# Key tiles of 128 tokens instead of 112, through device memory

## Chip, cores and metric

The kernel runs on one core of a Trainium2 chip. The time is device microseconds (us) of one execution; less is better.

## What is computed

The input is 32 images of 56 x 56 pixels with 32 channels. Three parts follow each other, each with a residual sum:

```python
x = x + conv(binarize(batchnorm(groupnorm(x))))        # 3 x 3, weights reduced to their signs
t = tokens(x)                                          # 3136 tokens of 32 channels an image
t = t + attention(layernorm(t))
t = t + experts(layernorm(t))                          # best 2 of 8, weighted

# attention, 16 heads of 32:
q = elu(n @ wq.T + bq) + 1;  k = elu(n @ wk.T + bk) + 1;  v = n @ wv.T + bv
kv_cos = sum over tokens of (k * cos)^T v;  kv_sin = sum over tokens of (k * sin)^T v
out = (q * cos @ kv_cos + q * sin @ kv_sin) / (q * cos . sum(k * cos) + q * sin . sum(k * sin) + 1e-5)
out @ dense.T + dense_b
```

The sum over tokens in kv_cos and kv_sin is the part that the change cuts anew: a sum does not care in which order or in which tiles the tokens come.

## The kernel before

**Tiles.** An image's 3136 tokens are kept as four groups g (the parity of row and column), each of 7 tiles of 112 tokens: 28 slots of 112. Token tiles lie with 112 partitions; channel tiles lie with 4 x 32 = 128 partitions.

**Stages.** Five engines each walk a list of steps; step kinds have short names, and a step n of image m waits on semaphores for what it reads. For one image: XT turns the loaded pixels to channels on partitions (DVE makes the signs in `nat`); CV shifts `nat` by DMA and convolves; XC centres and turns back to tokens; POOL's PN1 makes the normed tokens `xn` (L785 and L789); ZT turns `xn` on PE in two halves, ACT keeps the fp16 high part and DVE the low part (L684, L971), and the queue of SP copies the parts into the four partition groups of `z1`, 16 DMAs in SBUF (L470).

K (L551) is 14 steps an image, each two matmuls of 112 tokens against 512 key columns; ACT makes the exponential (L688) and DVE the elu (L975) into `kbuf`, of which there are two. KX (L560) is 14 steps, each two fp32 matmuls of `xcs` (the normed tokens times cos and sin, made by POOL's CS, L797, from `xn`) with `kbuf`; it adds up over the image in one PSUM bank. G and `KT` make the small matrices from it. Then Q, DN, SU, R, RP, NM and T2 (queries, denominators, numerators, L576 to L624), PN2 and ZU (the second norm, with 16 more DMAs into `z2`), LG (router), RT and GT (gates), F (experts: L636, DVE's product L1058, three POOL sums L841 to L847) and OUT.

**Order.** The order of the steps is a table, worked out by a planner beforehand. `ORDER` gives each engine, for each step kind, a time for each n in units of which 14 are one image; `iteration` sorts an engine's steps by that time modulo 14, with the image that each belongs to, and that list repeats for each image. The times fix only the order within one engine: an engine that waits holds back everything behind it in its list. PE's results go through three PSUM slots of two banks (K, Q, R, RP, F, ...) and one bank (XT, CV, DN, NM, T2, ...); a slot is reused when its reader is done. The queue of SP has its own list: OUT, ZT, CV, XT (load of the next image), ZU.

**Opening.** Group norm and batch norm need sums over all images. SP loads all 32 images in 8 pieces of four into two stage buffers (L423, L429), PE turns them (L495), DVE gathers statistics (L891), and a chain over PE, DVE and POOL makes the thresholds. Then all weights (L433) and tables (L439) are loaded, and before its list PE waits for `act_pre`, which ACT sets after it has written a folded weight into `p2` (L654), itself after all tables are in. POOL waits for all weights and tables and prepares the fp16 weights.

## Time and profile before

| | us |
|---|---|
| median of 3 runs | 2426.46 |
| lowest and highest | 2424.11, 2431.5 |
| profiled execution, its own time | 2426.23 |
| its span, first to last instruction | 2424.4 |
| mean granted clock of TensorE | 0.961 of full speed |

The span is cut from the first to the last instruction of the core; the time of the execution has 1.8 us around it. PE is TensorE's matmuls, PEld its weight loads, DVE VectorE, ACT ScalarE, POOL GpSimd, SPq the queue of SyncE, which only issues DMAs. L551 is line 551 of the kernel.

### The profile page before, as it was taken

The numbers are of one execution on the slowest core, as the hardware profiler recorded it, in microseconds if no ns is written. First come the engines' busy times: TensorE is split into PE (matmuls) and PEld (weight loads), VectorE is DVE, ScalarE is ACT, GpSimd is POOL, SyncE is SP. The second block draws the span as 40 slices with busy tenths as digits, with TensorE's granted clock in tenths as the row PEclk, the third lists the DMA queues.
The fourth block names the chain that finished last, engine by engine and source line by source line (L and its number), as shares of the span: only waits on it lengthen the run. The fifth ranks groups of instructions, "written<-read, shape, count | busy, mean of one in ns | idle before, by whom it ended". The sixth has DMA issues, their size and how long they took to land.

```text
span 2424.4 us, 45391 instructions
## 1 busy us (share of the span) xinstructions
PE 2252.8 (93%) x15908; PEld 1126.0 (46%) x15908; DVE 2064.4 (85%) x2725; ACT 1589.9 (66%) x2789; POOL 1841.0 (76%) x1553
## 2 busy tenths in 40 slices
PE   4369999999999999999999999999999999999971
PEld 4324444444544444444544444454544444454441
DVE  5357899999999999999999999999999999998852
ACT  0157777777777777777777777777777777777620
POOL 0414588888888888888888888888888888888775
PEclk8589999999999999999999999999999999999985
DMA  7421112222221112222221212222211212211001
GB/s 209 112 39 22 32 29 44 35 42 45 45 44 34 36 34 43 34 44 44 45 42 36 34 37 40 35 45 45 45 39 37 37 36 40 36 38 35 21 21 27
DMA packets 284863, 105.31 MB, mean 43 GB/s; under 512 B 246032, under 2 KB 279680, under 8 KB 284512
## 3 DMA queue, kind: packets, MB, share of 16 engines
q1 hardware_dynamic: 284640, 102.41, 21.3%
q8 instruction: 131, 2.15, 0.4%
q14 instruction: 92, 0.75, 0.1%
HBM read 31.19 MB, written 12.85 MB: 18 GB/s over the span
## 4 chain that ended last, share of the span: by engine, by line
PE 67%; DVE 15%; ACT 6%; issue 5%; POOL 3%; DMA 2%; SPq 1%; POOLq 0%; DVEq 0%; ACTq 0%
PE ps L560 15%; PE ps L611 12%; PE ps L551 7%; PE ps L602 6%; PE ps L576 5%; PE ps L585 5%; DVE qbuf L981 4%; DVE prod L1058 4%; ACT ebuf L693 3%; DVE kbuf L975 3%; PE ps L542 2%; PE ps L535 2%; PE ps L630 2%; DVE den L993 2%; PE ps L530 2%
## 5 line engine op out<-in xcount | busy, mean ns | idle before, releaser
L975 DVE SCALAR_TENSOR_TENSOR kbuf<-ps,ebuf 112x1024 f32<-112x1024 f32 x448 | 546.2, 1219 | 114.3 <-ACT ebuf L688 111.8
L693 ACT ACTIVATE ebuf<-ps,small 128x896 f32<-128x896 f32 x448 | 450.3, 1005 | 195.0 <-PE ps L576 113.1
L688 ACT ACTIVATE ebuf<-ps,small 112x1024 f32<-112x1024 f32 x448 | 498.3, 1112 | 107.4 <-PE ps L551 87.8
L981 DVE SCALAR_TENSOR_TENSOR qbuf<-ps,ebuf 128x896 f32<-128x896 f32 x448 | 486.5, 1086 | 43.2 <-ACT ebuf L693 38.7
L802 POOL TENSOR_TENSOR qbuf<-spread_r,qbuf 128x896 f32<-128x896 f32 x224 | 469.0, 2094 | 21.4 <-ACT spread_r L725 21.4
L560 PE MATMUL ps<-kbuf,xcs 112*64 112x512 f32 x1792 | 474.9, 613 | 4.1 <-DVE kbuf L975 4.1
L785 POOL TENSOR_TENSOR rstd<-varr,power 112x28 f32<-112x28 f32 x64 | 307.2, 4800 | 137.7 <-DVE varr L960 137.5
L611 PE MATMUL ps<-qbuf,gmat 128*64 128x224 f32 x3584 | 390.1, 360 | 3.0 <-POOL qbuf L802 2.2
L611 PEld LDWEIGHTS ps<-qbuf,gmat 128*64 128x64 f32 x3584 | 243.7, 138 | 165.0 <-issue 77.8
L1058 DVE TENSOR_TENSOR prod<-ps,gate 112x1024 f32<-112x1024 f32 x224 | 271.2, 1212 | 29.6 <-POOL ffn L847 10.1
L551 PE MATMUL ps<-wk,z 128*112 128x512 f16 x896 | 280.1, 395 | 15.7 <-issue 12.6
L841 POOL TENSOR_TENSOR prod<-prod 112x512 f32<-112x512 f32 x224 | 285.5, 1275 | 1.5 <-DVE prod L1058 1.4
L725 ACT ACTIVATE spread_r<-ps 128x896 f32<-128x896 f32 x224 | 204.6, 913 | 82.2 <-PE ps L602 53.8
L576 PE MATMUL ps<-z,wq 128*128 128x448 f16 x896 | 245.5, 356 | 6.2 <-DVE qbuf L981 3.3
L602 PE MATMUL ps<-rs,sel 128*128 128x448 f16 x896 | 240.8, 357 | 10.5 <-ACT rs L719 4.3
L996 DVE TENSOR_TENSOR qbuf<-ps,qbuf 128x896 f32<-128x896 f32 x224 | 237.3, 1083 | 7.2 <-PE ps L602 4.6
L585 PE MATMUL ps<-qbuf,dmat 128*32 128x448 f32 x1792 | 231.9, 549 | 0.2
L551 PEld LDWEIGHTS ps<-wk,z 128*112 128x112 f16 x896 | 93.6, 129 | 206.7 <-DVE qbuf L981 74.0
L844 POOL TENSOR_TENSOR prod<-prod 112x256 f32<-112x256 f32 x224 | 163.4, 730 | 17.6
L560 PEld LDWEIGHTS ps<-kbuf,xcs 112*64 112x64 f32 x1792 | 101.7, 136 | 146.5 <-issue 116.1
L636 PE MATMUL ps<-we,z 128*112 128x256 f16 x896 | 145.0, 287 | 11.2 <-DVE prod L1058 10.4
L636 PEld LDWEIGHTS ps<-we,z 128*112 128x112 f16 x896 | 97.1, 133 | 83.3 <-issue 24.1
(131 smaller groups left out, 3052.6 us busy)
## 6 DMA issues: line engine op xcount, KB each, us to landing
z<-zhl SPq DMA_DIRECT2D x1024, 49.0 KB, 1.9
qbuf<-in_x SPq DMA_DIRECT2D x8, 1568.0 KB, 8.9
xt<-in_x SPq DMA_DIRECT2D x256, 49.0 KB
out<-ffn SPq DMA_DIRECT2D x256, 49.0 KB
shifted<-nat SPq DMA_DIRECT2D x128, 52.6 KB, 5.0
qbuf<-in_sel SPq DMA_DIRECT2D x1, 1024.0 KB, 13.2
tabn<-in_tabnc SPq DMA_DIRECT2D x1, 784.0 KB, 12.5
p<-in_p2c SPq DMA_DIRECT2D x1, 528.0 KB, 9.6
```

The lines of the kernel that those rows point to most:

```text
L551: mm = pe.matmul(o[0:PT, k, :], z1[:, m.par, s % G, s // G, :], wk16[:, :], start=True, stop=True)
L560: mm = pe.matmul(kt_bank[64 * k:64 * k + 64, :], xcs[:, 2 * n + k, :, :].rearrange("p a c -> p (a c)"), kbuf[:, n % 2, DH * k:DH * k + DH] ...
L576: mm = pe.matmul(o[:, k, 0:G * PT].rearrange("p (g t) -> p g t", g=G), wq16[:, 128 * (k0 + k):128 * (k0 + k) + 128], z1[:, m.par, :, j, :] ...
L585: mm = pe.matmul(o[32 * j:32 * j + 32, 0:HW4], dmat[:, m.par, c, :, :].rearrange("p a h -> p (a h)"), qbuf[:, c, 4 * h + j, :], start=(c = ...
L602: mm = pe.matmul(o[:, k, 0:HW4], sel16[:, 128 * a:128 * a + 128], rs[:, j // 4, :], start=True, stop=True)
L611: mm = pe.matmul(o[64 * v:64 * v + 64, 0:2 * PT].rearrange("p (a t) -> p a t", a=2), gmat[:, m.par, c, :, :].rearrange("p a o -> p (a o)") ...
L688: act.activation(ebuf[0:PT, 0, :].rearrange("p (a b) -> p a b", a=2), o[0:PT, :, :], ACT.Exp, bias=minus_one[0:PT, :]).then_inc(kexp_made, 1)
L693: act.activation(ebuf[:, 1, 0:2 * G * PT].rearrange("p (a b) -> p a b", a=2), o[:, :, 0:G * PT], ACT.Exp, bias=minus_one).then_inc(qexp_ma ...
L802: nc.gpsimd.tensor_tensor(qbuf[:, 2:4, n, :], spread_r[:, :, :], qbuf[:, 2:4, n, :], ALU.mult)\
L975: v.scalar_tensor_tensor(kbuf[:, n % 2, :].rearrange("p (a b) -> p a b", a=2), o[0:PT, :, :], 1.0, ebuf[0:PT, 0, :].rearrange("p (a b) -> ...
L981: v.scalar_tensor_tensor(qbuf[:, k0:k0 + 2, j, :], o[:, :, 0:G * PT], 1.0, ebuf[:, 1, 0:2 * G * PT].rearrange("p (a b) -> p a b", a=2), AL ...
L1058: v.tensor_tensor(prod[:, n % 2, :, :].rearrange("p s (e c) -> p (s e) c", c=C), o[0:PT, :, :].rearrange("p k (s c) -> p (k s) c", c=C), g ...
```

## The change

Keys are made in tiles of 128 tokens: 25 tiles (the last of 64) in 13 steps instead of 28 tiles of 112 in 14. `z1` lies with its tokens in one row, so K takes any 128 of them. KX needs `xcs` in the same tiles, but `xn` has 112 tokens on its partitions: a new step CS of SP writes `xn` to device memory (`xd`, four DMAs) and reads it back as 128-token tiles (`xkt`, two DMAs), and POOL multiplies `xkt` in place of `xn`, in parts of 12 and 13 tiles.

`z1` and `z2` are filled through device memory: one DMA writes both parts to `zd`, SP waits until it has landed, and four DMAs read it.

In the opening the images come in 16 pieces of two into four buffers; image 0 is loaded for XT right behind them; five weights get a semaphore of their own (`folds_in`); PE no longer waits for `act_pre` and the tables before its list, and ACT writes `p2` before its first ZT.

All lists of `ORDER` are new, of all engines; the diff is cut to what matters here.

```diff
+KT = -(-TOKENS // 128)
+KREST = TOKENS - 128 * (KT - 1)
+KS = (KT + 1) // 2
+KH = 6
...
-        "K": [-4.59, -3.99, -3.46, -2.65, -2.50, -1.33, -0.36, 0.73, 1.31, 2.08, 3.37, 3.87, 5.38, 6.72],
-        "KX": [-3.61, -3.01, -2.64, -1.63, -1.35, 1.00, 1.35, 2.48, 2.91, 3.66, 5.41, 6.26, 6.84, 7.25],
-        "ZT": [-10.56, -8.66],
+        "Q": [0.42, 2.60, 3.30, 4.56, 5.99, 6.42, 6.69, 7.14, 8.03, 8.58, 9.61, 10.19, 11.90, 12.80],
+        "K": [-5.95, -4.14, -3.65, -2.80, -2.20, -1.05, 0.46, 1.20, 1.76, 2.94, 3.46, 3.68, 4.66],
+        "KX": [-3.79, -3.27, -2.28, -1.90, -0.98, 0.61, 2.35, 3.02, 3.24, 3.48, 4.65, 5.65, 6.40],
+        "RP": [10.77, 11.26, 12.00, 14.85, 19.71, 20.00, 20.68],
+        "R": [10.98, 13.69, 13.90, 15.54, 19.72, 19.98, 20.60],
+        "NM": [12.46, 16.51, 17.47, 20.23, 20.51, 20.77, 24.20],
+        "ZT": [-10.34, -7.59],
+        "T2": [19.83, 20.95, 21.71, 24.36],
+        "G": [6.80, 6.90],
+        "F": [34.99, 35.66, 36.49, 37.53, 38.78, 40.49, 41.98],
...
     "gpsimd": {
-        "CS": [-1.95, 6.49],
-        "PN1": [-4.03],
+        "CS": [2.80, 5.54],
+        "PN1": [-7.59],
...
     "sync": {
-        "OUT": [42.36],
-        "ZT": [-9.43],
-        "CV": [-23.34],
-        "XT": [-35.15],
-        "ZU": [24.07],
+        "CS": [-17.68, -12.90],
+        "CV": [-23.27],
+        "XT": [-36.85],
+        "ZU": [19.44],
+        "OUT": [39.11],
+        "ZT": [-14.92],
...
-        stage = [qflat[0:PT, k * 3584:(k + 1) * 3584].rearrange("p (b f) -> p b f", b=4) for k in range(2)]
+        stage = [qflat[0:PT, k * 1792:(k + 1) * 1792].rearrange("p (b f) -> p b f", b=2) for k in range(4)]
...
+        zd = [nc.dram_tensor(f"zd{k}", [128, 2, PATCHES], F16).ap() for k in (1, 2)]
+        z_out = [sem(f"z_out{k}") for k in (1, 2)]
+        xd = nc.dram_tensor("xd", [TOKENS, C], F32).ap()
+        xkt_out = sem("xkt_out")
+        xkt_in = sem("xkt_in")
...
-            x4 = x.rearrange("(q b) h w c -> q b (h w c)", b=4).rearrange("q b (p f) -> q p b f", p=PT)
-            for k in range(2):
-                sp.dma_start(stage[k], x4[k]).then_inc(stage_in[k], 16)
+            x2 = x.rearrange("(q b) h w c -> q b (h w c)", b=2).rearrange("q b (p f) -> q p b f", p=PT)
+            for q in range(4):
+                sp.dma_start(stage[q], x2[q]).then_inc(stage_in[q], 16)
...
-            for q in range(2, 8):
-                sp.wait_ge(stage_turned, 4 * q - 4)
-                sp.dma_start(stage[q % 2], x4[q]).then_inc(stage_in[q % 2], 16)
-            for dst, src in ((views["taps"], conv_taps), (views["valid"], validc), (wva_s, wv[0]), (wvb_s, wv[1]), (wd_s, wd),
-                             (views["wqa"], wq[0]), (wqb_s, wq[1]), (views["wka"], wk[0]), (wkb_s, wk[1]),
-                             (views["wea"], we[0]), (web_s, we[1])):
-                sp.dma_start(dst, src).then_inc(weights_in, 16)
...
+            for q in range(4, B // 2):
+                sp.wait_ge(stage_turned, 2 * q - 6)
+                sp.dma_start(stage[q % 4], x2[q]).then_inc(stage_in[q % 4], 16)
...
+            load(Img(None, 0))
+            for dst, src in ((views["taps"], conv_taps), (views["valid"], validc), (wva_s, wv[0]), (wvb_s, wv[1]), (wd_s, wd)):
+                sp.dma_start(dst, src).then_inc(folds_in, 16)
+            for dst, src in ((views["wka"], wk[0]), (wkb_s, wk[1]), (views["wqa"], wq[0]), (wqb_s, wq[1]),
+                             (views["wea"], we[0]), (web_s, we[1])):
+                sp.dma_start(dst, src).then_inc(weights_in, 16)
...
-                if kind == "XT" and n == 0:
+                if kind == "XT" and n == 0 and m.c > 0:
                     wait(sp, xres_made, m.at(2))
                     load(m)
...
                     sp.wait_ge(zlow_made[ln], m.at(2, 2))
+                    wait(sp, z_in[ln], m.at(64))
+                    sp.dma_start(zd[ln], zhl[ln][:, :, :]).then_inc(z_out[ln], 16)
+                    sp.wait_ge(z_out[ln], m.at(16, 16))
+                    src = zd[ln].rearrange("(g c) h f -> h c g f", g=G)
                     for r in range(4):
-                        for g in range(G):
-                            dst = z2[32 * r:32 * r + 32, g] if ln else z1[32 * r:32 * r + 32, m.par, g]
-                            sp.dma_start(dst.rearrange("p j t -> p (j t)"),
-                                         zhl[ln][32 * g:32 * g + 32, r % 2, :]).then_inc(z_in[ln], 16)
+                        dst = z2[32 * r:32 * r + 32] if ln else z1[32 * r:32 * r + 32, m.par]
+                        sp.dma_start(dst.rearrange("p g j t -> p g (j t)"), src[r % 2]).then_inc(z_in[ln], 16)
+                if kind == "CS" and n == 0:
+                    sp.wait_ge(xn_made[0], m.at(1, 1))
+                    wait(sp, xkt_in, m.at(32))
+                    for g in range(G):
+                        dst = xd[PATCHES * g:PATCHES * g + PATCHES].rearrange("(j t) c -> t j c", t=PT)
+                        src = xn[0][:, :, :].rearrange("p (j g) c -> p g j c", g=G)[:, g]
+                        sp.dma_start(dst, src).then_inc(xkt_out, 16)
+                if kind == "CS" and n == 1:
+                    sp.wait_ge(xkt_out, m.at(64, 64))
+                    wait(sp, xcs_made, m.at(2))
+                    sp.dma_start(xkt[:, 0:KT - 1, :], xd[0:128 * (KT - 1)].rearrange("(i p) c -> p i c", p=128)).then_inc(xkt_in, 16)
+                    sp.dma_start(xkt[0:KREST, KT - 1, :], xd[128 * (KT - 1):TOKENS]).then_inc(xkt_in, 16)
...
-            for q in range(8):
-                pe.wait_ge(stage_in[q % 2], 16 * (q // 2) + 16)
-                for b in range(4):
-                    if 4 * q + b >= 4:
-                        pe.wait_ge(stage_read, 4 * q + b - 3)
-                    for j in range(TILES):
-                        dst = ps[:, 2 * b + (j >= 4), (j % 4) * PT:(j % 4 + 1) * PT]
-                        mm = pe.transpose(dst, stage[q % 2][:, b, j * 128:(j + 1) * 128], eye[0:PT, 0:PT])
-                    mm.then_inc(stage_turned, 1)
+            for img in range(B):
+                q, b = img // 2, img % 4
+                pe.wait_ge(stage_in[q % 4], 16 * (q // 4) + 16)
+                if img >= 4:
+                    pe.wait_ge(stage_read, img - 3)
+                for j in range(TILES):
+                    dst = ps[:, 2 * b + (j >= 4), (j % 4) * PT:(j % 4 + 1) * PT]
+                    mm = pe.transpose(dst, stage[q % 4][:, img % 2, j * 128:(j + 1) * 128], eye[0:PT, 0:PT])
+                mm.then_inc(stage_turned, 1)
...
-            pe.wait_ge(weights_in, 16 * 11)
+            pe.wait_ge(folds_in, 16 * 5)
...
-                    pe.wait_ge(z_in[0], m.at(256, 256))
+                    pe.wait_ge(z_in[0], m.at(64, 64))
                     if n == 0:
                         pe.wait_ge(weights_made, 1)
-                    for k in range(2):
-                        s = 2 * n + k
-                        mm = pe.matmul(o[0:PT, k, :], z1[:, m.par, s % G, s // G, :], wk16[:, :], start=True, stop=True)
+                    flat = z1[:, m.par, :, :, :].rearrange("p g j t -> p (g j t)")
+                    for k in range(2 if n < KS - 1 else 1):
+                        a, w = 128 * (2 * n + k), 128 if 2 * n + k < KT - 1 else KREST
+                        mm = pe.matmul(o[0:w, k, :], flat[:, a:a + w], wk16[:, :], start=True, stop=True)
                     mm.then_inc(ring_full, 1)
                 elif kind == "KX":
-                    pe.wait_ge(k_made, m.at(14, n + 1))
-                    if n in (0, 7):
-                        pe.wait_ge(xcs_made, m.at(2, n // 7 + 1))
+                    pe.wait_ge(k_made, m.at(KS, n + 1))
+                    if n in (0, KH):
+                        pe.wait_ge(xcs_made, m.at(2, n // KH + 1))
                     if n == 0:
                         wait(pe, kt_copied, m.at(1))
-                    for k in range(2):
-                        mm = pe.matmul(kt_bank[64 * k:64 * k + 64, :],
-                                       xcs[:, 2 * n + k, :, :].rearrange("p a c -> p (a c)"),
-                                       kbuf[:, n % 2, DH * k:DH * k + DH], start=(n == 0), stop=(n == 13))
+                    for k in range(2 if n < KS - 1 else 1):
+                        i = 2 * n + k
+                        w = 128 if i < KT - 1 else KREST
+                        mm = pe.matmul(kt_bank[64 * k:64 * k + 64, :], xcs[0:w, i, :, :].rearrange("p a c -> p (a c)"),
+                                       kbuf[0:w, m.at(KS, n) % 2, DH * k:DH * k + DH], start=(n == 0), stop=(i >= KT - 2))
                     mm.then_inc(ktx_done, 1)
...
-            pe.wait_ge(act_pre, 1)
             pe.wait_ge(dve_pre, 6)
-            pe.wait_ge(tables_in, 16 * 9)
...
-            act.wait_ge(tables_in, 16 * 9)
-            act.wait_ge(pe_pre, 3)
-            for v in range(2):
-                for cs in range(2):
-                    q = slice(64 * v + 32 * cs, 64 * v + 32 * cs + 32)
-                    dst = p2[q, :, cs, :, 0:C]
-                    last = act.activation(dst, ps[q, 2, :].rearrange("p (a h o) -> p a h o", a=CH, h=HPC), ACT.Copy,
-                                          scale=SHIFT)
-            last.then_inc(act_pre, 1)
...
+                    if m.c == 0 and n == 0 and kind == "ZT":
+                        act.wait_ge(tables_in, 16 * 9)
+                        act.wait_ge(pe_pre, 3)
...
                     wait(pool, high_made[ln], m.at(2))
+                    if not ln:
+                        wait(pool, xkt_out, m.at(64))
                     nc.gpsimd.tensor_tensor(xn[ln][:, :, 0:C - 1], xc[ln][:, :, 0:C - 1],
                                             rstd[ln][:, :].unsqueeze(2).to_broadcast([PT, SLOTS, C - 1]), ALU.mult)\
                         .then_inc(xn_made[ln], 1)
                 elif kind == "CS":
-                    pool.wait_ge(xn_made[0], m.at(1, 1))
-                    wait(pool, ktx_done, m.at(14, 7 * n - 7))
-                    w = slice(14 * n, 14 * n + 14)
+                    pool.wait_ge(xkt_in, m.at(32, 32))
+                    wait(pool, ktx_done, m.at(KS, 0 if n else KH - KS))
+                    w, c = (slice(2 * KH, KT), KT - 2 * KH) if n else (slice(0, 2 * KH), 2 * KH)
                     for k in range(2):
-                        last = nc.gpsimd.tensor_tensor(xcs[:, w, k, :], xn[0][:, w, :],
-                                                       tabk[:, k, w].unsqueeze(2).to_broadcast([PT, 14, C]), ALU.mult)
+                        last = nc.gpsimd.tensor_tensor(xcs[:, w, k, :], xkt[:, w, :],
+                                                       tabk[:, k, w].unsqueeze(2).to_broadcast([128, c, C]), ALU.mult)
                     last.then_inc(xcs_made, 1)
                 elif kind == "RP":
```

## Rows read from the trace of the kernel before

**Rows 1.** Part 1 of the page: busy us, share of the span, instructions.
```profile
PE 2252.8 (93%) x15908; PEld 1126.0 (46%) x15908; DVE 2064.4 (85%) x2725; ACT 1589.9 (66%) x2789; POOL 1841.0 (76%) x1553
```

**Rows 2.** Windows of the first 110 us and of 400 us inside.
```profile
core 0: us, PE busy (x) PEld busy (x) DVE busy (x) ACT busy (x) POOL busy (x), PEclk, DMA share, GB/s
0.00:110.00 110.00, 51.31 (x293) 46.41 (x293) 51.24 (x140) 6.65 (x11) 16.51 (x18) 0.70 0.67 176
...
1200.00:1600.00 400.00, 398.58 (x2838) 194.82 (x2836) 368.04 (x473) 289.77 (x495) 335.79 (x283) 1.00 0.21 39
```

**Rows 3.** Windows of one period, one image passing each engine.
```profile
1200.00:1268.30 68.30, 68.08 (x491) 33.51 (x489) 62.91 (x82) 49.52 (x88) 57.00 (x49) 1.00 0.21 41
```

**Rows 4.** Groups by line, whole run: busy us, mean ns, idle before.
```profile
L975 DVE SCALAR_TENSOR_TENSOR kbuf<-ps,ebuf 112x1024 f32<-112x1024 f32 x448 | 546.2, 1219 | 114.3 <-ACT ebuf L688 111.8
L560 PE MATMUL ps<-kbuf,xcs 112*64 112x512 f32 x1792 | 474.9, 613 | 4.1 <-DVE kbuf L975 4.1
L611 PE MATMUL ps<-qbuf,gmat 128*64 128x224 f32 x3584 | 390.1, 360 | 3.0 <-POOL qbuf L802 2.2 <-DVE pbuf L1002 0.5 <-ACT mean L737 0.2
L551 PE MATMUL ps<-wk,z 128*112 128x512 f16 x896 | 280.1, 395 | 15.7 <-issue 12.6 <-DVE kbuf L975 2.4 <-DVE qbuf L981 0.5
L576 PE MATMUL ps<-z,wq 128*128 128x448 f16 x896 | 245.5, 356 | 6.2 <-DVE qbuf L981 3.3 <-ACT spread_r L725 1.3 <-DVE kbuf L975 1.1
L602 PE MATMUL ps<-rs,sel 128*128 128x448 f16 x896 | 240.8, 357 | 10.5 <-ACT rs L719 4.3 <-ACT spread_r L725 0.3
L636 PE MATMUL ps<-we,z 128*112 128x256 f16 x896 | 145.0, 287 | 11.2 <-DVE prod L1058 10.4 <-DVE qbuf L996 0.8
L624 PE MATMUL ps<-pair_sb,pbuf 128*112 128x66 f32 x896 | 116.0, 252 | 0.0
L622 PE MATMUL ps<-eye_mean,t1b 128*112 128x132 f32 x448 | 94.4, 293 | 5.9 <-DVE pbuf L1002 5.7
```

**Rows 5.** Timeline of PE: start us, us, instructions merged.
```profile
1254.09 1.08 PE L560 MATMUL ps<-kbuf,xcs 112*64 112x512 f32 x4
1255.10 0.64 PE L551 MATMUL ps<-wk,z 128*112 128x512 f16 x2
1255.58 0.54 PE L576 MATMUL ps<-z,wq 128*128 128x448 f16 x2
```

**Rows 6.** Timeline, second half of a ZT step to the next image's first K.
```profile
1249.78 0.51 PE L542 MATMUL ps<-eye_center,xn 112*128 112x112 f32 x3
1250.87 0.50 DVE L971 TENSOR_TENSOR zhl<-ps,zhl 128x336 f16<-128x336 f32 x1
1254.32 10.39 SPq L470 DMA_DIRECT2D z<-zhl  x16
1269.91 0.63 PE L551 MATMUL ps<-wk,z 128*112 128x512 f16 x2
```

**Rows 7.** DMA issues by line: KB each, median us from issue to landing.
```profile
qbuf<-in_x SPq DMA_DIRECT2D x8, 1568.0 KB, 8.9
z<-zhl SPq DMA_DIRECT2D x1024, 49.0 KB, 1.9
p<-in_p2c SPq DMA_DIRECT2D x1, 528.0 KB, 9.6
```

**Rows 8.** DMA queues in 1200 to 1268 us: packets, MB, share of 16 engines.
```profile
q1 hardware_dynamic: 9350, 2.67, 20.2%
```

**Rows 9.** Chain that ended last, opening: start us, us, what.
```profile
27.41 8.67 DMA qbuf<-in_x
...
71.41 0.39 PE ps L500 x2
...
82.91 1.28 ACT L654
...
86.64 1.02 PE ps L521 x4
...
118.04 12.61 issue
```

**Rows 10.** The same chain, last of the three z trips of the tail.
```profile
2384.52 1.91 DMA z<-zhl
```

More of the change, by code:

```diff
@@ L289, in build @@
         rstd = [sb(f"rstd{k}", [PT, SLOTS]) for k in (1, 2)]
-        xcs = sb("xcs", [PT, SLOTS, 2, C])
+        xkt = sb("xkt", [128, KT, C])
+        xcs = sb("xcs", [128, KT, 2, C])
         z1 = sb("z1", [128, 2, G, TILES, PT], F16)
@@ L347, in build @@
         eye_in = sem("eye_in")
-        stage_in = [sem(f"stage_in{k}") for k in range(2)]
+        stage_in = [sem(f"stage_in{k}") for k in range(4)]
         stage_turned = sem("stage_turned")
@@ L686, in step @@
                     act.wait_ge(ring_full, no + 1)
[L687 to L689 removed]
+                    wait(act, k_made, m.at(KS, n))
+                    w, c = (128, 2) if n < KS - 1 else (KREST, 1)
+                    act.activation(ebuf[0:w, 0, 0:DH * c].rearrange("p (a b) -> p a b", a=c), o[0:w, 0:c, :], ACT.Exp,
+                                   bias=minus_one[0:w, :]).then_inc(kexp_made, 1)
                 elif kind == "Q":
@@ L867, in _ @@
             v.memset(nat[:, :, :], 1.0)
+            v.memset(xkt[:, KT - 1:KT, :], 0.0)
             v.memset(dmat[:, :, :, :, :], 0.0)
@@ L984, in step @@
                 elif kind == "DN" and n % 4 == 3:
+                    if m.c == 0 and n == 3:
+                        dve.wait_ge(tables_in, 16 * 9)
                     h = n // 4
```

90 lines of the change are left out of this document (58 added, 32 removed), and 70 rows, old and new, of the table ORDER.

## Prediction

> **What bounds the kernel now.** I read the page's busy shares first, then windows of busy time by stage, then one period, then the groups by line, the timeline around the steps that change, and the chain through opening and tail. PE is busy for 93% of the span [rows 1], but that is a mean over stages: in the first 110 us it is busy for less than half of the time, and inside the run for 398.6 of 400 us at full granted clock [rows 2]. One period of 68.3 us, in which each engine does one image's worth of steps, holds 68.1 us of PE, 62.9 of DVE, 57.0 of POOL and 49.5 of ACT [rows 3]. So work taken from PE should shorten the period, one for one, as long as nothing that PE waits for comes later than today. Opening and tail are chains of waits, and there other things count.
>
> **K and KX (steady).** The 28 token tiles of 112 become 25, the last of half height: 14 steps become 12 whole and one half, so 1.5 steps of each kind go. Mean times go with the columns moved, 356 ns for 448 against weights of 128 x 128 and 395 for 512 against 128 x 112 [rows 4], so I take 128 tokens instead of 112 as free. Whole-run groups give 474.9 us for 448 KX steps, 1.06 each, and 280.1 for 448 K steps, 0.63 each [rows 4]; there neighbours overlap. From start to start, a KX takes 1.01 us and the K behind it 0.48 [rows 5]. I take 1.01 and, between 0.48 and 0.63, 0.55: 1.5 x 1.56 = 2.34 us an image. At most it is 1.5 x 1.69 = 2.5, at least 1.5 x 1.49 = 2.2. Nearly all images pass in steady state; with 31 periods that is 72 us (69 to 79). DVE loses 1.5 x 1.22 = 1.8 us an image with them [rows 4], and ACT about as much; both lie beside PE, so they add nothing, but they keep DVE's share where it is, 61.1 us in a period of 66.0. POOL's CS takes 100 columns' worth instead of 112, a gain off the path.
>
> A rule speaks against this reading. The Trainium skill (Perfetto Trace Analysis, Identifying the Most-Contended Engine) says that matmul busy time is no measure of TensorE's headroom, and to take the most occupied engine otherwise. By that rule DVE is the bound and the term is 57 us, not 72: it stands as a rival below.
>
> **The z trip.** Today the second half of ZT ends at 1250.3 us, DVE's low part at 1251.4, SP's 16 issues take 10.4 us from 1254.3 on, landing 1.9 later, at 1266.6, and the first K comes at 1269.9: 3.3 us spare [rows 6, 7]. The trip alone is 12.3 us. The new one is a write of 392 KB, a wait for its landing, and four reads of 196 KB. The trace has no landing of a write to device memory. From rows 7, 1519 KB more take 7.0 us more to land, 217 KB a us: the write lands 1.9 + 343 / 217 = 3.5 us after its issue of 0.6, the reads 1.9 + 735 / 217 = 5.3 after theirs. That is 10.0 us, 2.3 less than now. With the 1.1 us of ACT and DVE, z is there 11.1 us after ZT.
>
> But the new order also puts the first K much closer to ZT. Between them stand on PE four Q, two NM, an R, an RP, two F, two T2 and two small G. By rows 4 (the two lines of T2 together) that is 4 x 0.55 + 2 x 1.74 + 2 x 0.54 + 2 x 0.65 + 2 x 1.64 = 11.3 us, G left out; a tenth less if they overlap as K does in rows 5, 10.2. The middle, 10.8, leaves z 0.3 us late an image, 9 us in all. As bounds: if every hop lands like today's small ones, 1.1 + 0.6 + 1.9 + 2.4 + 1.9 = 7.9, and nothing is late. If the write lands like the 528 KB load that took 9.6 us behind others, 7.1 us for its size, the trip is 14.7 and 3.9 late. I stay near the first, as in steady state the queue is mostly idle [rows 8].
>
> The Trainium skill (DMA: Bandwidth & Descriptors, Anatomy of one DMA) says of the GpSimd path that most of a DMA's fixed time is the receipt of the written bytes, heaviest for device memory. No run here shows it; it speaks for the late end.
>
> **The xn trip.** Six DMAs and a wait of SP. The rows are 128 bytes, some 3136 written and as many read an image. In a period 9350 packets take 20.2% of 16 engines [rows 8], 23.5 ns each; 6272 more are 147 us, 9 us on each engine, so the share goes from 0.20 to about 0.34: no bound. In latency: `xn` is written as soon as POOL has it, before ZT; the read is queued on SP behind OUT and the z trip, and between first K and first KX PE has another K, an NM, two F and three Q, 0.63 + 1.74 + 1.3 + 1.65 = 5.3 us by rows 4, besides the denominators. POOL's CS comes behind three F sums there. I put it at nothing; if that cover goes, each us is 31 in all. Queued behind the waiting SP are CV, XT and ZU; SP's 10.4 us of z issues shrink to 3.0 and a wait of 3.5, twice an image, so the list as a whole has more room than before.
>
> **Opening.** The statistics are done at 71.4 us, behind loads of 8.7 us each that alternate with PE's turning [rows 9]. Sixteen pieces in four buffers keep loads in flight: 12544 KB at 217 KB a us are 58 us, with 3 to start and 3 to finish, 64. I take 7 us off; halving the waits of 8.7, three on the chain, would give 13, and if memory bounds already, nothing. PE starts its list 3.7 us after ACT's write of `p2` begins [rows 9] and no longer waits for it; how long DVE's chain still holds it isn't on these rows, so 2 of 0 to 3.7. The first image waits 12.6 us for z [rows 9], 2.3 to 2.9 of which go. Together 11 (2 to 20).
>
> **Tail.** Three z trips lie on the chain, the last landing at 2386.4 [rows 10]; at 2.3 each 7, of which two stand partly beside POOL's sums: 5 (0 to 9).
>
> **Sum.** Against the profiled execution's own 2426.2 (span 2424.4 and 1.8 around it; 0.3 under the median of the runs, so no correction): 2426 - 72 - 11 - 5 + 9 = **2347 us**.
>
> **Rivals.**
> - **DVE sets the period.** For it: 62.9 of 68.3 us, waits for ring slots that DVE frees. Against: PE's gaps are 0.2 us a period. The steady term is 57: 2362 us.
> - **A trip misses its cover a little.** z or `xkt` 1.2 us late an image, PE idle ahead of the first K or KX: 2426 - 88 + 37 = 2375 us. For it: the two estimates differ by less than their error.
> - **A loop through POOL and SP holds the period.** CS now waits for a read behind OUT and ZT on SP, and POOL's list stands still meanwhile, RL and RP behind it; the period stays 68.3 and only opening and tail gain: 2410 us. Against: POOL has 11 us a period spare [rows 3].
> - **Slower: the write to device memory lands late.** At 3.9 us late an image: 2426 - 88 + 121 = 2459 us. It decides from 2.8 us on, a trip of 13.6 us after ZT; the 9.6-us landing is the only row for it, taken in the crowded opening.
>
> **Chances.** The forecast has 0.50, with its own range 2318 (79 for the steps, 20 and 9 for the ends, nothing late) to 2361; DVE 0.13, the small miss 0.17, the loop 0.08, the late write 0.09, and 0.03 for gains that cancel. The range takes in the first three, with the small miss up to 2.1 us an image (2426 - 88 + 65 = 2403): 2318 to 2403, 0.79 together. About 0.3%, 7 us, is what a measurement can tell from no change. The first four cases are faster by more (0.87, after a little for their edges), 0.03 within, 0.10 slower.
>
> **What would show it.** Right: K groups of 800 matmuls and KX of 1600, a period near 66.3 us with PE still over 99% busy, the statistics' matmul near 64 us, z landing 10 to 11 us after ZT. Wrong: PE idle ahead of the first K with a z load as releaser (late trip), ahead of the first KX with POOL's `xcs` (loop or `xkt`), or DVE above 95% with PE's share down (DVE). The forecast is wrong if the period is not below 67.5 us.

## The result, and the profile after

The change makes the kernel faster, by about a quarter of what was forecast: 2404.97 us (2403.08 to 2406.63) against 2425.89 (2424.11 to 2431.5), ratio 0.9904 with a 95% interval of 0.989 to 0.9918. That is 21 us less, where 79 were forecast, and 2 us above the upper end of the stated range, 2403. The profiled execution has a span of 2403.2 us.

Part 1 of the page of the changed kernel (busy us, share, instructions):

```profile
PE 2183.1 (91%) x15620; PEld 1098.5 (46%) x15620; DVE 2062.3 (86%) x2694; ACT 1516.3 (63%) x2757; POOL 1839.2 (77%) x1553
```

TensorE has lost 69.7 us of busy time against [rows 1], almost the 72 of the steady term. VectorE, which has 1.5 clamps an image fewer, has lost 2. The windows over the same stretches as [rows 2, 3] (columns: length, then busy us of PE, PEld, DVE, ACT and POOL, granted clock, DMA share, GB/s):

```profile
0.00:110.00 110.00, 54.89 (x303) 47.42 (x303) 50.64 (x143) 8.55 (x15) 22.86 (x19) 0.72 0.70 180
1200.00:1268.30 68.30, 65.88 (x482) 32.74 (x480) 62.87 (x80) 47.20 (x87) 56.99 (x49) 1.00 0.36 63
```

In the same 68.3 us TensorE is busy for 65.88 us where it was for 68.08: 2.2 less, and 2.4 us idle where there were 0.2. So the question is why the period did not follow. That it did not is read from GpSimd's power step, which each image makes twice. Columns: start, duration, the instruction, and in brackets the wait before it. First the changed kernel, the same step of two images in the steady part, then the first and the last but one of the run; below it the kernel before, the first and the last but one:

```profile
99.73 4.81 POOL L819 TENSOR_TENSOR rstd<-varr,power 112x28 f32<-112x28 f32 x1 [14.19 <-DVE varr L996]
...
1209.77 4.80 POOL L819 TENSOR_TENSOR rstd<-varr,power 112x28 f32<-112x28 f32 x1 [1.38 <-DVE varr L996]
...
1278.06 4.80 POOL L819 TENSOR_TENSOR rstd<-varr,power 112x28 f32<-112x28 f32 x1 [1.39 <-DVE varr L996]
...
2296.25 4.80 POOL L819 TENSOR_TENSOR rstd<-varr,power 112x28 f32<-112x28 f32 x1
```
```profile
109.90 4.80 POOL L785 TENSOR_TENSOR rstd<-varr,power 112x28 f32<-112x28 f32 x1 [18.16 <-DVE varr L960]
...
2307.50 4.80 POOL L785 TENSOR_TENSOR rstd<-varr,power 112x28 f32<-112x28 f32 x1
```

The period is 1278.06 - 1209.77 = 68.29 us, as before. The first step is 10.2 us earlier, the last but one 11.3, the end 21.2. So the opening gave 10 us, all the periods between 1, the tail 10.

**Where TensorE waits.** Timeline of TensorE in one period: the four rows that have a wait over 0.1 us, and the second half of ZT (L572):

```profile
1238.57 0.55 PE L636 MATMUL ps<-rs,sel 128*128 128x448 f16 x2 [0.32 <-DVE qbuf L1018]
...
1244.04 0.51 PE L572 MATMUL ps<-eye_center,xn 112*128 112x112 f32 x3
...
1251.57 0.48 PE L656 MATMUL ps<-eye_mean,t1b 128*112 128x132 f32 x2 [1.39 <-DVE pbuf L1041]
...
1256.06 0.60 PE L582 MATMUL ps<-wk,z 128*128 128x512 f16 x2 [0.21 <-DVE qbuf L1018]
...
1258.28 0.55 PE L610 MATMUL ps<-z,wq 128*128 128x448 f16 x2 [0.16 <-DVE qbuf L1018]
```

The largest, 1.39 us, is T2's second step waiting for VectorE's numerators. VectorE and GpSimd just before it:

```profile
1248.33 1.08 DVE L1035 TENSOR_TENSOR qbuf<-ps,qbuf 128x896 f32<-128x896 f32 x1
1249.33 1.29 DVE L1086 TENSOR_SCALAR rmax<-rmax 112x28 f32<-112x28 f32 x1
...
1251.13 0.38 DVE L1041 TENSOR_TENSOR pbuf<-ps,tabn 128x224 f32<-128x224 f32 x1
```
```profile
1248.49 2.10 POOL L838 TENSOR_TENSOR qbuf<-spread_r,qbuf 128x896 f32<-128x896 f32 x1 [0.88 <-ACT spread_r L759]
```

L1086 adds 1 to 28 numbers. In the kernel before the same step took 0.17 us (its group there):

```profile
L1047 DVE TENSOR_SCALAR rmax<-rmax 112x28 f32<-112x28 f32 x10 | 1.7, 171 | 0.0
```

Here it takes 1.29 and ends at 1250.62, when GpSimd's multiply does (1250.59). The new lists put the last routing step (RT 5) beside GpSimd's last RP and ahead of the numerators. With L1071, 0.81 us where it was 0.38 and beside another RP, VectorE loses here 1.6 of the 1.8 us an image that the shorter K series gave it.

**The chain of waits** of one period, cut to its turns (start, us, what); the next period repeats it 68.28 us later:

```profile
1201.66 2.09 POOL qbuf L838
...
1209.77 4.80 POOL rstd L819
...
1222.85 4.80 POOL rstd L819
...
1234.54 1.00 POOL rs L850
...
1235.96 0.39 ACT rs L753
...
1238.57 0.55 PE ps L636 x2
...
1249.42 1.22 DVE rmax L1086
1250.66 0.34 DVE rmax L1088
1251.13 0.40 DVE pbuf L1041
1251.57 0.48 PE ps L656 x2
...
1269.95 2.09 POOL qbuf L838
```

It goes round through all four engines' fixed lists, and the part on TensorE is small: 25% of the page's whole chain, 35% GpSimd's. It isn't closed at every turn: ahead of the two power steps the full chain has 1.3 and 2.8 us that it calls "issue", and GpSimd's timeline puts these down to VectorE's `varr` (L996).

**The trips** of z and `xn` were not late. DMA issues (KB each, median us from issue to landing), and SyncE's issues of the z trip that belongs to the ZT above:

```profile
z<-zd SPq DMA_DIRECT2D x256, 196.0 KB, 3.8
zd<-zhl SPq DMA_DIRECT2D x64, 392.0 KB, 2.4
...
xd<-xn SPq DMA_DIRECT2D x128, 98.0 KB, 2.9
...
xkt<-xd SPq DMA_DIRECT2D x32, 384.0 KB, 6.6
```
```profile
1245.61 0.35 SPq L484 DMA_DIRECT2D zd<-zhl  x1
...
1248.39 2.68 SPq L489 DMA_DIRECT2D z<-zd  x4
```

The last read is issued by 1251.1 and lands some 3.8 us later, at 1254.9 (an estimate from the median); the first K (L582) starts at 1256.06 and waits only for VectorE. No row of TensorE waits for a z load in the steady part.

**Opening**, in the chain of waits: the statistics' matmul, the first XT, and the first image's `z` and `xkt` trips.

```profile
63.61 0.62 PE ps L530 x2
...
75.25 0.95 PE ps L551 x4
...
110.58 2.35 DMA zd<-zhl
115.21 7.42 DMA xkt<-xd
```

Against [rows 9] the statistics are 7.8 us earlier and XT 11.4. Then the read of `xkt`, a new link, keeps GpSimd and the first KX waiting.

### The profile page after: what moved, and what is told of

It is laid out like the page before. It is cut to its first block, busy times and chain, and to the rows that moved or that the text cites. A ratio compares the mean times of both kernels' runs of the same rounds, so it can differ in the third digit from the quotient of the medians.

```text
span 2403.2 us, 44296 instructions
## 1 busy us (share of the span) xinstructions
PE 2183.1 (91%) x15620; PEld 1098.5 (46%) x15620; DVE 2062.3 (86%) x2694; ACT 1516.3 (63%) x2757; POOL 1839.2 (77%) x1553
## 4 chain that ended last, share of the span: by engine, by line
POOL 35%; PE 25%; DVE 17%; ACT 10%; issue 10%; DMA 3%; SPq 0%; POOLq 0%; ACTq 0%; DVEq 0%
POOL rstd L819 11%; POOL qbuf L838 7%; DVE qbuf L1018 6%; POOL prod L877 5%; ACT ebuf L727 4%; PE ps L619 4%; POOL xn L825 4%; PE ps L645 3%; POOL prod L880 3%; PE ps L593 3%; PE ps L610 3%; PE ps L636 2%; ACT ebuf L722 2%; POOL xcs L833 2%; PE ps L658 2%
## 5 line engine op out<-in xcount | busy, mean ns | idle before, releaser
L1012 DVE SCALAR_TENSOR_TENSOR kbuf<-ps,ebuf 128x1024 f32<-128x1024 f32 (+1 forms) x416 | 487.6, 1172 | 48.2 <-ACT ebuf L722 44.7
L722 ACT ACTIVATE ebuf<-ps,small 128x1024 f32<-128x1024 f32 (+1 forms) x416 | 448.0, 1077 | 116.0 <-DVE kbuf L1012 68.2
L593 PE MATMUL ps<-kbuf,xcs 128*64 128x512 f32 (+1 forms) x1600 | 440.4, 611 | 7.7 <-DVE kbuf L1012 4.0
L582 PE MATMUL ps<-wk,z 128*128 128x512 f16 (+1 forms) x800 | 244.2, 384 | 23.4 <-issue 14.0
L1035 DVE TENSOR_TENSOR qbuf<-ps,qbuf 128x896 f32<-128x896 f32 x224 | 243.4, 1087 | 23.3 <-PE ps L636 20.0
L593 PEld LDWEIGHTS ps<-kbuf,xcs 128*64 128x64 f32 (+1 forms) x1600 | 101.2, 136 | 120.6 <-issue 74.6
L636 PEld LDWEIGHTS ps<-rs,sel 128*128 128x128 f16 x896 | 67.5, 99 | 182.3 <-issue 63.1
L717 ACT ACTIVATE zhl<-ps 128x448 f16<-128x448 f32 (+1 forms) x128 | 63.5, 497 | 134.5 <-PE ps L572 134.5
```

The lines of the kernel that those rows point to most:

```text
L593: mm = pe.matmul(kt_bank[64 * k:64 * k + 64, :], xcs[0:w, i, :, :].rearrange("p a c -> p (a c)"), kbuf[0:w, m.at(KS, n) % 2, DH * k:DH * k ...
L636: mm = pe.matmul(o[:, k, 0:HW4], sel16[:, 128 * a:128 * a + 128], rs[:, j // 4, :], start=True, stop=True)
L722: act.activation(ebuf[0:w, 0, 0:DH * c].rearrange("p (a b) -> p a b", a=c), o[0:w, 0:c, :], ACT.Exp, bias=minus_one[0:w, :]).then_inc(kexp ...
L1012: v.scalar_tensor_tensor(kbuf[0:w, m.at(KS, n) % 2, 0:DH * c].rearrange("p (a b) -> p a b", a=c), o[0:w, 0:c, :], 1.0, ebuf[0:w, 0, 0:DH * ...
```

## The experiments

All ratios are to the kernel before, by runs on the same chip. The period is read as above, the median over the steady images; TensorE's busy time is its share of the window 1000 to 1683 us times the period. e4, e6, e8, e9 and e14_old_less_nm have single images that are 2 to 3 us longer than the median.

| kernel | time, us | ratio (95%) | period | TensorE busy an image |
|---|---|---|---|---|
| before | 2425.9 | 1 | 68.30 | 68.1 |
| changed | 2405.0 | 0.9904 (0.989 to 0.9918) | 68.28 | 65.9 |
| e1_ratio_by_reduce | 2390.0 | 0.9843 (0.9828 to 0.9858) | 67.70 | 65.9 |
| e2_pbuf_first | 2389.2 | 0.9843 (0.9828 to 0.9857) | 67.74 | 66.0 |
| e3_g_twice | 2405.1 | 0.9905 (0.9891 to 0.992) | 68.30 | 66.3 |
| e4_old_fewer_keys | 2409.6 | 0.9924 (0.9904 to 0.9945) | 67.7 | 67.2 |
| e5_old_one_step_less | 2420.5 | 0.9969 (0.996 to 0.9978) | 68.1 | 67.0 |
| e6_z_by_sbuf | 2489.9 | 1.0246 (1.0227 to 1.0266) | 71.3 (69.0 to 73.7) | 67.2 |
| e7_28_moves | 2374.8 | 0.978 (0.9766 to 0.9795) | 67.14 | 66.0 |
| e8_34_moves | 2376.8 | 0.979 (0.9773 to 0.9807) | 67.25 | 65.7 |
| e9_old_less_pe | 2426.4 | 0.9995 (0.9985 to 1.0004) | 68.3 | 67.2 |
| e10_old_less_dve | 2426.4 | 0.9996 (0.9986 to 1.0005) | 68.30 | 67.9 |
| e11_new_less_pe | 2406.1 | 0.9915 (0.99 to 0.9929) | 68.29 | 64.8 |
| e12_new_less_dve | 2405.1 | 0.992 (0.9904 to 0.9937) | 68.30 | 65.9 |
| e13_old_z2_trip | 2416.6 | 0.9956 (0.9939 to 0.9972) | 68.30 | 68.1 |
| e14_old_less_nm | 2419.0 | 0.9957 (0.9942 to 0.9972) | 68.0 | 67.5 |
| e14_old_z2_trip_less_nm | 2401.0 | 0.9887 (0.9872 to 0.9901) | 67.75 | 67.2 |
| e15_new_less_nm | 2399.3 | 0.9879 (0.9864 to 0.9893) | 68.01 | 65.1 |
| **e16_45_moves** | **2345.4** | 0.9657 (0.9641 to 0.9674) | 66.26 | 65.4 |

### Is it the wait at T2, and is TensorE still the bound?

```
e1  -  v.tensor_scalar(w1, ratio, 1.0, None, ALU.add)
    +  v.tensor_reduce(w1, rmax[:, 6:8, :].rearrange("p k s -> p s k"), AX_X, ALU.add)   # rows: ratio, ones
e2  -  "RT": [34.41, 34.56, 35.49, 35.62, 35.65, 35.88],
    +  "RT": [34.41, 34.56, 35.49, 35.62, 35.65, 36.01],
e3  -  for k in range(2):          (G)
    +  for k in (0, 1, 0, 1):
```

> The changed kernel, with one VectorE step made in another form. In its profile the step that adds 1 to the expert ratio (28 numbers a partition) takes 1.29 us an image, against 0.17 us in the kernel before, and it ends when GpSimd's 2.1 us multiply beside it ends. Here the 1 comes from a sum over two rows, as a reduction, a form that stood beside GpSimd without a stall in the same profile (the piece sums, 0.36 us each). Theory A (a closed chain of waits through all the engines' fixed lists holds the period at 68.28 us, no engine's own work does): the step lies on the chain, so the period falls by up to 1.0 us, to about 67.3, and the time to about 2375. Rival B (VectorE's own work is the bound): the same, 2375. Rival C (TensorE is still the bound): 2405, no change. Should the step keep its 1.3 us, the stall is not one of its form.

> The changed kernel, with one entry of VectorE's order moved: the last routing step (5) stands behind the sixth numerator's multiply in place of ahead of it. No engine's work changes. In the changed kernel's profile TensorE waits 1.39 us there in every image. Theory A (chain of waits): TensorE's wait falls to a few tenths, and the period by what the next longest chain leaves, between 0 and 1.3 us: 2365 to 2405. Rival B (VectorE's own 62.9 us are the bound): its work is the same, so 2405. Rival C (TensorE's work is the bound): 2405.

> The changed kernel, with each of the 16 matmuls of both G steps made twice, into the same place: 0.67 us more TensorE work an image, just ahead of the place where TensorE waits 1.39 us for VectorE in every image. Theory A and rival B: the wait takes it up, 2405, within 3 us. Rival C (TensorE is still the bound): 32 x 0.67 = 21 us more, 2426.

e1 and e2 each give 15 us and 0.54 to 0.58 us of the period; e3 gives nothing either way, so TensorE had room for 0.67 us more an image (0.4 in its busy time), and rival C falls. In e1 half of the stall goes and half moves on to the next step that reads only SBUF (VectorE's timeline of e1; L1091 had 0.19 us in the changed kernel):

```profile
1243.00 0.20 DVE L1087 TENSOR_REDUCE rmax<-rmax 112x28 f32<-112x56 f32 x1
...
1243.60 0.70 DVE L1091 TENSOR_TENSOR rmax<-rmax 112x28 f32<-112x28 f32 x1
```

In e2 the 1.39 us at T2 are gone, and a new wait stands at the next step (TensorE's timeline of e2):

```profile
1244.53 0.64 PE L670 MATMUL ps<-we,z 128*112 128x256 f16 x4 [0.72 <-DVE qbuf L1018]
```

This is the pattern of all that follows: a cause is found, and taking it away gives less than its own length, because another chain is nearly as long. Of rival B one thing stood open: in e1 and e2 VectorE's busy time falls by 0.6 us, as much as the period.

### Did the old lists let a gain through?

e4 shortens the last three K and KX steps of the kernel before by half, e5 the last one to 8 columns:

```
e4  -  for k in range(2):                  (K, KX; the exponential and the clamp with them)
    +  for k in range(2 if n < 11 else 1):
e5  +  w = DH if n < 13 else 8             (columns of K, KX, exponential and clamp)
```

> The kernel before with its own orders, where the last three K steps of an image make one tile of keys in place of two (three of the 28 tiles of 112 tokens are left out of the sum over keys): 1.5 K and 1.5 KX less for TensorE, which is what the change saves, and the exponentials and clamps of ScalarE and VectorE shortened with it. Nothing else of the change is in. If TensorE was the bound before and the old lists let the gain through: 31 x 2.3 = 72 us less, 2354. If the old lists too hold a chain near 68 us by themselves: less than 15 us, 2411 or more.

> The kernel before with its own orders and re-tiling nowhere, where the last K step and the last KX step of an image work on 8 columns in place of 512 (two of the 28 tiles of keys are left out of the sum): one whole K and one whole KX less for TensorE, and the clamp and the exponential of that step cut short. It mends the run before it, in which halves of KX steps were left out: their two matmuls stand in different halves of TensorE's columns and run side by side (502 records took 148.1 us, as did 560 in the kernel before), so a half saves nothing and that run had only 0.6 us less to do. If TensorE's work was the bound before and the old lists let a gain through: 1.0 + 0.4 = 1.4 us an image less, 31 x 1.4 = 43 us, 2383. If the old lists hold 68 us of their own: 2411 or more.

e4 missed its 2354 because the price of its edit was wrong. The groups of KX over ten images, e4 first, the kernel before below:

```profile
L560 PE MATMUL ps<-kbuf,xcs 112*64 112x512 f32 x502 | 148.1, 609 | 0.0
```
```profile
L560 PE MATMUL ps<-kbuf,xcs 112*64 112x512 f32 x560 | 147.7, 610 | 0.0
```

A tenth of the matmuls gone, and the same busy time. A KX step's two matmuls write different halves of the partitions and run side by side, so half a step costs a whole one. That holds for the change too: it saves one KX an image, not 1.5. In its own groups over ten images a whole KX step takes 1.05 us (125.9 for 120) and the half one 1.07 (10.7 for 10):

```profile
L593 PE MATMUL ps<-kbuf,xcs 128*64 128x512 f32 x480 | 125.9, 607 | 0.0
L593 PE MATMUL ps<-kbuf,xcs 64*64 64x512 f32 x20 | 10.7, 614 | 0.0
```

e4's period fell by 0.6 us all the same, TensorE's busy time by 0.8. It cut 2.0 us of VectorE's busy time too, and which of the two paid is not parted. e5 removes a whole K and KX, and of 1.4 us (1.05 in busy time) the period gives up 0.2; TensorE waits 0.76 us an image for VectorE at two Q steps, where the kernel before shows no wait. The old lists too hold 68.1 us by something else than TensorE.

### Are the new lists at fault, and do they need the new trip?

```
e6  -  sp.dma_start(zd[ln], zhl[ln][:, :, :]) ... four reads
    +  for r in range(4):
    +      for g in range(G):
    +          sp.dma_start(dst[r, g], zhl[ln][32 * g:32 * g + 32, r % 2, :])
e7, e8   28 and 34 entries of ORDER, no other line
```

> The changed kernel, with z spread again by the 16 copies from SBUF to SBUF of the kernel before, in place of one write to device memory and four reads; all else, the new orders too, as changed. If the new trip is worth nothing in the steady part and about 2.5 us in the opening and 3 in the tail: 2410. If the new orders count on its earlier landing: the 16 issues of 0.6 us keep the queue 9.6 us where the new trip keeps it 5.5, z comes some 1 to 2 us late in every image, and the time is 2435 to 2470. If the new trip costs time (rival: its load on the DMA engines slows other transfers), the time falls below 2400.

> The changed kernel with 28 entries of its orders moved by one to ten places (8 of TensorE, 7 of VectorE, 3 of ScalarE, 10 of GpSimd), and no other edit: the same instructions, the same transfers. The places are worked out from the durations in the changed kernel's rows so that TensorE's list waits for nobody. Theory A (the lists, not an engine's work, hold the period): it falls from 68.28 to 66 to 66.6, TensorE's work of 65.9 us being the next bound, and the time to 2335 to 2355. Rival B (VectorE's own work with its hand-overs): its work stays 62.9 us, so the time stays within 15 us of 2405.

> The same as the run of 28 moves, with another set of 34 moved entries, found independently: 9 of TensorE, 6 of VectorE, 2 of ScalarE and 17 of GpSimd or so. Theory A: 2335 to 2355 again, since no single place but the absence of waits on TensorE matters. Rival B: 2390 to 2405.

e6: 85 us slower than the changed kernel, past the late end of what was expected. The z copies of one image on SyncE's queue, and the first K on TensorE's timeline, in the steady part of e6:

```profile
1217.23 10.41 SPq L486 DMA_DIRECT2D z<-zhl  x16
```
```profile
1229.07 0.59 PE L580 MATMUL ps<-wk,z 128*128 128x512 f16 x2 [1.51 <-issue]
```

The last copy is issued by 1227.6, and K starts 1.4 us behind it, after 1.5 us of waiting for which the profile names no releaser.

That lateness is the smaller part of the 85 us. From 700 to 1180 us the images wait 1.2 to 1.4 us there, and the period is 69.0 to 69.1, 0.8 above the changed kernel's. In most others the wait is 1.7 to 2.9 us, TensorE's granted clock falls behind it to 0.50, the lower of its two levels (1.2 GHz), for some 3 us, and the period is 71.1 to 73.7. In the changed kernel the clock is 1.00 through the steady part. One such image of e6, TensorE's K and the windows ahead of it and behind it:

```profile
459.94 0.59 PE L580 MATMUL ps<-wk,z 128*128 128x512 f16 x2 [2.08 <-issue]
```
```profile
454.00:456.00 2.00, 2.00 (x20) 1.84 (x19) 1.34 (x3) 0.77 (x5) 1.48 (x3) 1.00 0.28 70
462.00:464.00 2.00, 2.00 (x14) 1.17 (x14) 1.82 (x2) 0.14 (x1) 0.48 (x2) 0.50 0.53 53
```

So the shorter z trip is real, and the new lists have already spent it: in the changed kernel z lands 1.2 us ahead of K, and a trip some 2 us longer is late in every image. Nothing was left to gain from the trip as such. e7 and e8 take 30 and 28 us off the changed kernel with the same instructions, half of what was expected and twice what rival B allowed. They also free VectorE of the L1086 stall (0.17 us in both), so they don't yet part the lists from VectorE's work.

### One engine's work at a time

```
e9, e11    -  for k in range(4):              (CV)
           +  for k in range(1):
e10, e12   -  v.tensor_scalar(nat[:, a:a + w * YL, 1:1 + PR], o[:, 0:w * PT]...
           +  v.tensor_scalar(nat[:, a:a + 1, 1:1 + PR], o[:, 0:PR]...
```

> The kernel before, where the convolution makes one of its four matmuls for each half image (three of four taps groups are left out of the convolution): 1.28 us less TensorE work an image (0.95 to 0.24 and 0.76 to 0.19), nothing less for any other engine, in a step that is made two images ahead. Theory P (TensorE's work was the bound, as the prediction had it): 32 x 1.28 = 41 us less, 2386. Theory D (VectorE's busy time plus some 5.5 us of hand-over waits an image is the bound: the period less VectorE's busy time came to 5.4 to 5.7 us in the kernel before, the changed one and the four runs on its lists): within 8 us of 2427. Theory L (chains through both lists): between them.

> The kernel before, where VectorE compares one image row in place of 16 and of 12 with the threshold (the rest of the signs is left out): about 1.1 us less VectorE work an image (0.75 to 0.15 and 0.62 to 0.15), nothing less for any other engine, in a step two to three images ahead. Theory P: 2427, within 5. Theory D: 31 x 1.1 = 34 us less, 2393. Theory L: between them.

> The changed kernel with the convolution cut to one matmul in four (three of four taps groups left out): 1.28 us less TensorE work an image and nothing else less. TensorE waits 2.4 us an image here already. Theory P: 41 us less, 2364. Theory D: 2400 to 2405. Theory L: some 10 to 25 us less.

> The changed kernel with VectorE's comparison cut to one row of each half image (the rest of the signs left out): about 1.1 us less VectorE work an image and nothing else less. Theory P: 2405. Theory D: 31 x 1.1 = 34 us less, 2371. Theory L: some 10 to 25 us less.

Four times nothing, less than theory L too gave for e11 and e12 (10 to 25 us). Neither TensorE's work (theory P) nor VectorE's (theory D) is the bound, in either kernel, where these two steps stand. The cuts were smaller than priced: by its groups the convolution lost 1.05 us an image and not 1.28, VectorE's comparison 0.76 and not 1.1. What TensorE is spared goes into new waits. In e9 every image has two of them, 0.8 us together, for VectorE's clamp of K close behind the shortened convolution. The second z trip is waited for too, but in 5 of 20 images only (TensorE's timeline of e9):

```profile
1215.76 0.55 PE L576 MATMUL ps<-z,wq 128*128 128x448 f16 x2 [0.35 <-DVE kbuf L975]
1218.45 0.55 PE L576 MATMUL ps<-z,wq 128*128 128x448 f16 x2 [0.45 <-DVE kbuf L975]
...
1244.86 1.58 PE L630 MATMUL ps<-we,z 128*112 128x8 f16 x28 [0.67 <-DMA z<-zhl]
```

In e11 two waits for the same clamp appear, 1.1 us for the 1.05 taken away, and the rest of the period is as it was:

```profile
1202.00 0.55 PE L636 MATMUL ps<-rs,sel 128*128 128x448 f16 x2 [0.63 <-DVE kbuf L1012]
1205.85 0.55 PE L610 MATMUL ps<-z,wq 128*128 128x448 f16 x2 [0.48 <-DVE kbuf L1012]
```

### The second chain of the kernel before

```
e13        the second z trip by zd: one write, four reads; the first as it was
e14, e15   -  for c in range(CH):             (NM)
           +  for c in range(CH - (n in (1, 2, 3))):
```

> The kernel before with its own lists, where the second z trip alone (for the experts' input) goes by one write to device memory and four reads, as in the change, in place of 16 copies. Theory P (TensorE's list alone held 68.3 us; the trip was hidden): the steady part stays at 68.3, only the last image's trip is shorter, by about 3 us: 2424. Theory Z (a closed chain through that trip, as long as TensorE's list, held it as well): the period falls to what TensorE's list needs, 68.1 us at 99.7% busy: 31 x 0.2 = 6 us and the 3 us of the tail, 2418.

> The kernel before with its own lists and its own z trips, where the numerator steps 1, 2 and 3 sum three of the four groups of heads (a quarter of these sums is left out): 3 x 4 matmuls, 3 x 0.41 = 1.24 us less TensorE work an image, nothing less for another engine. Theory P: 32 x 1.24 = 40 us less, 2387. Theory Z: the period stays where the z2 trip's chain holds it, 2410 to 2427, and TensorE's waits grow by what its work lost.

> Both edits: the kernel before with the second z trip through device memory and with 1.24 us less TensorE work in the numerator steps 1 to 3. Theory P: 2387 less 3 in the tail, 2384. Theory Z with this one chain alone beside TensorE's list: 40 + 9 us less, 2378. Theory L (more chains of nearly the same length through both lists): the period falls in part, to 67.3 to 68, 2395 to 2415.

> The changed kernel with the same cut: numerator steps 1, 2 and 3 sum three of the four groups of heads, 1.24 us less TensorE work an image. In the changed kernel's chain of waits TensorE does not stand on the chain in this stretch (it goes by GpSimd's list there), but TensorE runs through the stretch without a wait. Theory G (the loop through GpSimd's list alone holds 68.28 us): 2405. Theory L (TensorE's list from its second SU to its fourth NM, with the waits behind it, is a chain of nearly the same length): in part, 10 to 25 us less, 2380 to 2395. Theory P: 40 us less, 2365.

e13 alone leaves the period at 68.30, as theory P had it; its 11 us (0.0044 of 2428) come from the ramps at both ends, more than the 3 us of the tail that either theory gave. Of 1.24 us less TensorE work the kernel before turns 0.27 into period with its own z trip, 0.55 with the shorter one, the changed kernel 0.27.

The first 0.27 is a median over two kinds of images. In e14_old_less_nm TensorE's router step (L631) waits for the second z trip in 19 of 30 images, 0.2 to 0.9 us. From 1041 to 1516 us it doesn't, and there the period is 67.76, as with the shorter trip (67.75), where no router step waits in the steady part. One image of either kind:

```profile
974.17 1.58 PE L631 MATMUL ps<-we,z 128*112 128x8 f16 x28 [0.64 <-DMA z<-zhl]
...
1109.19 1.56 PE L631 MATMUL ps<-we,z 128*112 128x8 f16 x28
```

So the second z trip is a chain of its own, and the rest of the 1.24 us is held by another. Theory Z alone is wrong (it wanted nothing in the first and all in the second), P and G too. What stands is L in its direction: TensorE's list, the z trip and at least one more chain lie within about 0.5 us of each other, so work on one buys the distance to the next. Its size it missed in e15, 6 us less than the changed kernel where 10 to 25 were expected.

### The lists alone

Part of e16's edit, the GpSimd list, to two places; 45 entries in all:

```
-  "F": [42.27, 43.77, 43.78, 45.54, 46.63, 48.87, 49.45],
-  "T2": [26.63, 27.91, 29.24, 31.66],
...
-  "RP": [18.59, 18.65, 20.27, 22.09, 24.52, 25.13, 26.70],
+  "F": [45.30, 45.41, 46.30, 46.82, 47.38, 47.70, 49.45],
+  "T2": [26.63, 32.31, 32.56, 33.36],
...
+  "RP": [19.36, 19.38, 20.27, 22.09, 24.52, 25.13, 30.50],
```

> The changed kernel with a third set of places: 45 entries of its orders moved (18 of TensorE, 7 of VectorE, 5 of ScalarE, 15 of GpSimd), no other edit. Above all GpSimd's last multiply of an image (RP 6) goes behind the gate in place of ahead of it, so that VectorE's routing step no longer stands behind it, and its expert sums go later. Theory L (several closed chains of nearly the same length; the lists decide how much of TensorE's saved work comes out): the period falls from 68.28 to between 66.5 and 67.1 us, the time to 2350 to 2375. If the runs of 28 and 34 moves had already met another bound: 67.1 again, 2375 or more.

2345 us, past the fast end of what was expected: 60 us under the changed kernel and 82 under the one before, with the changed kernel's own instructions and transfers. One period of it, as a window:

```profile
1200.00:1266.30 66.30, 65.41 (x483) 32.32 (x482) 61.72 (x81) 47.45 (x87) 56.87 (x49) 1.00 0.40 65
```

TensorE is busy for 65.4 of 66.3 us. So the change's operations can run at this pace, and its lists were what held them at 68.28: shown, since nothing else differs. Which of the 45 places count for how much was not tried. e2, which moves RT 5 alone, got 0.54 us; e16 leaves RT 5 where it was and moves GpSimd's multiply away from it, after which L1086 takes 0.17 us again. No run gave the kernel before such new places, so how much of the 2.0 us is the change's work and how much the better lists is open.

## Why the prediction was wrong

- **"Work taken from PE should shorten the period, one for one, as long as nothing that PE waits for comes later than today."** This step failed: 2.2 us less TensorE work left the period at 68.29, and 45 other places in the lists made it 66.26. What TensorE waits for did come later (VectorE's numerators, 1.39 us), in lists that the change had rewritten. And one for one did not hold even with the old lists: e5, e9 and e14_old_less_nm got 0.2, 0 and 0.27 us for 1.4, 1.05 and 1.24; only e4 got most of its own (0.6 of 0.8 busy us), with less work for VectorE beside it. The 68.1 busy us [rows 3] were read as a bound. They were one of several chains of nearly equal length; the second z trip was another. The prediction looked for what would be late next only along the transfers it had seen change, not along VectorE's list.
- **1.5 K + 1.5 KX, 2.34 us.** TensorE's busy time fell by 2.2, so the sum looked right, but by two errors that cancel, which is luck. Half a KX saves nothing, and the groups of KX fell by 1.08 us an image (474.9 to 440.4 over 32), not 1.52; those of K fell by 1.12 (280.1 to 244.2), not 0.83. By the prediction's own start-to-start rows the term would have been 1.01 + 0.55 for the whole steps and some 0.2 for the half K, 1.8 us, or 55 us in place of 72. e16's period is 2.04 us shorter than that of before, and that its 2345 us lie 2 from the forecast's 2347 is luck again: 63 us in place of 72, and nothing for a late z.
- **z trip.** The mechanism was right: z was forecast 11.1 us behind ZT and came 10.3 behind it (1244.6 to 1254.9); a write that lands after 2.4 us, not 3.5, and reads after 3.8, not 5.3. The cover was 11.5 us, not 10.8, but 1.6 of it are TensorE's waits for VectorE; its work there is 9.9 us, and without these waits z would have been 0.4 late (an estimate from these rows). So the 9 us for lateness were not paid here, and the rival of a late write, with its 3.9 us, found no row.
- **xn trip.** Nothing in the steady part, as forecast, with the DMA share at 0.36 against about 0.34. In the opening the read of `xkt` stands on the chain (7.4 us), which the prediction had not looked for; it ate what was ahead of it (XT 11.4 us earlier, the first KX 9.7).
- **Opening -11, tail -5.** 10 and 10: the opening was nearly right, the tail's gain twice what was forecast. The statistics were forecast at 64 and stand at 63.6. In the tail the trip is 8.3 us on the chain, from the issue at 2357.0 to the logits at 2365.3.
- **Rivals.** The time is that of the third, a loop through POOL and SP that holds the period at 68.3, 2410, which had 0.08. Its outcome was right and its place not: `xcs` waits for the read only in the opening, and the loop went by RP, the VectorE step that stood still beside it, and the order of steps behind it; e1 and e2, which change or move that step, get 0.54 to 0.58 us, so it is a part of the loop and not all. "POOL has 11 us a period spare" was no argument against it, since in a closed chain spare time elsewhere on the engine does not help.
- **The Trainium skill's rule** that matmul busy time is no measure of headroom (Trainium skill, Perfetto Trace Analysis, Identifying the Most-Contended Engine): the trace agrees, as 1.05 us of matmuls less changed nothing at 99.7% busy (e9). Its alternative, that VectorE as the most occupied engine is the bound, is not borne out: 0.76 us less there changed nothing either (e10, e12).

## What to carry to other kernels

In a software pipeline with fixed lists per engine, a high busy share doesn't say that the engine's work is the bound: cut a little of it away from a step that nobody needs soon, and see whether the period moves. Before pricing an edit, look for the other closed chains (follow what repeats after exactly one period) and take as its gain the distance to the next. When the lists are rewritten with the edit, price them apart from it: here the same operations ran with a period 2.0 us shorter than before, 63 us in all, on one set of lists, and no shorter on another.
